# GpSimd's bias add behind the second power, VectorE's final add last in its step

## The chip, the core and the metric

The kernel runs on one core of one Trainium2 chip. The metric is device time in microseconds; before the change the median of three runs is 1020.15 us (1020.0 to 1021.33).

## What is computed

32 sequences of 512 tokens go through one block of a small language model with 256 channels:

```python
h = weight[x] * keep_mask[x]                       # gather 512 rows of 256, masked
# mixer on n1 = layernorm(h)
u, res = split(n1 @ in_proj_w.T)                   # 512 and 256 channels
u = conv1d(u, conv_w, 4 taps, causal) + conv_b
delta = softplus(u @ dt_proj_w.T + dt_proj_b)
g = u * sigmoid(delta)
y = scan(state = 0.9 * state + 0.1 * g)            # over the tokens
h = h + (y @ out_proj_w.T + res)
# quantised linear layer on n2 = layernorm(h)
xd = mx_quantise(n2)                               # blocks of 32, fp6 grid, dequantised
h = h + (xd @ wd.T + ffn_bias)
```

## The kernel before

Everything is float32. A product is made from three matmuls in fp32r: high part by high part, high by the low part of the weights, and the low part of the data by high. So each operand x of a product needs x_hi (a copy by ScalarE) and x_lo = x - x_hi (a subtraction, mostly on GpSimd: L370 for g, L377 for u, L407 for xT; VectorE makes nT_lo, L874).

The kernel is a software pipeline over the sequences, with an order written out by hand for every engine. Each engine has a function step(st) that is called for s = 0 to 33. In step s the "main" part works on sequence s (in_proj, convolution, dt_proj, gate), the "back" part on s - 1 (out_proj, scan, merge into h2, second norm, quantisation), the "tail" part on s - 2 (dequantise, turn by a DMA round trip through DRAM, linear product, bias, result, store). "front" prepares n1 of s + 1, "early" the statistics of s + 2. Engines wait for each other by semaphores only; each runs its own queue in order. Steps 2 to 29 have all of these parts; 30 has no "early" part, 31 neither "early" nor "front".

The places that matter here, by engine in the order of a step:

- GpSimd: first power (L384) and L386, g_lo[3] of s - 1 (L370), gathers, u_lo[0] and u_lo[1] (L377), gathers, **add_bias (L402)**, u_lo[2], u_lo[3], xT_lo (L407), second power inverse_root2 (L393, L396), g_lo[0] to g_lo[2].
- VectorE: dequantise (L769), turn_blocks (L862), gate(3) of s - 1 (L791), convolve (L707), turn_n1 (L869), scan (L799), convolve, add_h (L717) and statistics2, variance2 (L731, L734, L735), statistics1 (L838), variance1 (L845, L850, L851), gate(0), gate(1), **add_linear (L784)**, split_nT (L874), block_max (L740), quantise (L746, L754, L760), gate(2).
- ScalarE: taps, u_hi (L488), xT_hi (L550), tanh (L492), the second norm (L541, which waits for L396), g_hi (L499).
- TensorE: in_proj(0), (1), out_proj, in_proj(2), (3), dt_proj of m = 0, 1 for k = 0, 1 (L1026, L1027, L1033), merge (L1010 to L1017), dt_proj of m = 0, 1 for k = 2, 3, the linear product (L1070 to L1072, which waits for xT_lo), dt_proj(2) (its PSUM bank must have been read by gate(0)), dt_proj(3).

add_bias adds the bias in place to h2 of sequence s - 2; it waits for n2_ready of the step before (the norm has read h2). add_linear adds the linear product from PSUM (psO) to the same h2; it waits for bias_added and f_psum and releases result_ready, on which the output DMA of SyncE and the next step's merge wait.

Of the kernel before, what the change touches and what calls it, by code (L numbers as in the profile page):

```python
# [54 lines left out]
def lm_tower_kernel(nc, x, table, in_wT, conv_w, conv_b, dt_wT, dt_b, out_wT, ffn_w, ffn_b, turned, out):  # L55
# [13 lines left out]
    with ExitStack() as ctx:  # L69
# [131 lines left out]
        def f32(ap):  # L201
            return ap.bitcast(F32)
# [4 lines left out]
        def by_token(xT_part):  # L207

            return flat(xT_part).rearrange("p (m a i) -> p m a i", a=Q, i=BLOCK)

        def later(v):

            return not isinstance(v, int) or v > 0
# [32 lines left out]
        def span(part):  # L246

            return slice(0, C) if part is None else slice(part * C // 2, (part + 1) * C // 2)
# [8 lines left out]
        def linear_psum(st):  # L257


            return psZ_chunks if st.back and not st.main else psO  # L260
# [16 lines left out]
        def steps(eng, step):  # L277

            first = RING
            for s in range(0, first):  # L280
                step(Step(s, s % RING, s // RING))
            turns = (NSEQ - first - 2) // RING
            with eng.Fori(0, turns) as turn:
                for r in range(first, first + RING):
                    step(Step(RING * turn + r, r, turn + r // RING))
            for s in range(first + RING * turns, NSEQ + 2):
                step(Step(s, s % RING, s // RING))
# [54 lines left out]
        @block.gpsimd  # L342
        def _(pool):
            pool.memset(ident[:], 0.0).then_inc(zeroed, 1)
            pool.memset(decay[:], DECAY).then_inc(const_ready, 1)
            pool.memset(neg_half[:], -0.5).then_inc(const_ready, 1)
            pool.wait_ge(zeroed, 1)
            pool.affine_select(out=ident[:], in_=ident[:], compare_op=ALU.not_equal, fill=1.0, base=0,
                               pattern=[[-1, P]], channel_multiplier=1).then_inc(ident_ready, 1)

            def gather(b, ring, chunks):

                for c in chunks:
                    at = bass.IndirectOffsetOnAxis(ap=ids[:, b, c:c + 1], axis=0)
                    pool.indirect_dma_start(out=rows[:, ring, c, :], out_offset=None, in_=table,  # L355
                                            in_offset=at).then_inc(gathered[ring], 16)

            for n in range(2):
                pool.wait_ge(ids_loaded[n], 16)
                gather(n, n, range(C))  # L360
            pool.wait_ge(const_ready, 2)

            def step(st):
                s = st.s

                def split_g(m, s):
                    pool.wait_ge(g_hi_ready[m], s + 1)
                    if m == 0 and later(s):
                        pool.wait_ge(o_psum[1], s)
                    pool.tensor_tensor(g_lo[:, m, :], g[:, m, :], f32(g_hi[:, m, :]),  # L370
                                       ALU.subtract).then_inc(g_lo_ready[m], 1)

                def split_u(m):
                    pool.wait_ge(u_hi_ready[m], s + 1)
                    if m == 0 and later(s):
                        pool.wait_ge(z_psum[M - 1], s)
                    pool.tensor_tensor(u_lo[:, m, :], u[:, m, :], f32(u_hi[:, m, :]),  # L377
                                       ALU.subtract).then_inc(u_lo_ready[m], 1)

                def inverse_root1():  # L380
                    pool.wait_ge(var1_ready, s + 2)
                    if later(s + 1):
                        pool.wait_ge(n1_ready, s + 1)
                    pool.tensor_tensor(rstd1[:], ve1[:], neg_half[:], ALU.pow).then_inc(rstd1_ready, 1)  # L384
                    pool.wait_ge(rstd1_ready, s + 2)
                    pool.tensor_tensor(nmr1[:], nm1[:], rstd1[:], ALU.mult).then_inc(nmr1_ready, 1)  # L386

                def inverse_root2(part):
                    cs = span(part)
                    pool.wait_ge(var2_ready, s + (part or 0))  # L390
                    if later(s - 1):
                        pool.wait_ge(n2_ready, s - 1)
                    pool.tensor_tensor(rstd2[:, cs], ve2[:, cs], neg_half[:, cs],  # L393
                                       ALU.pow).then_inc(rstd2_ready, 1)
                    pool.wait_ge(rstd2_ready, s + (part or 0))
                    pool.tensor_tensor(nmr2[:, cs], nm2[:, cs], rstd2[:, cs], ALU.mult).then_inc(nmr2_ready, 1)  # L396

                def add_bias():
                    for part in st.tail_parts:
                        pool.wait_ge(n2_ready, s - 1 + (part or 0))  # L400
                        cs = h2[:, st.b, span(part)]
                        pool.tensor_tensor(cs, cs, bias[:].unsqueeze(1).to_broadcast([P, cs.shape[1], D]),  # L402
                                           ALU.add).then_inc(bias_added, 1)

                def split_xT():
                    pool.wait_ge(xT_hi_ready, s - 1)
                    pool.tensor_tensor(by_token(xT_lo[:]), xT_by_token, f32(by_token(xT_hi[:])),  # L407
                                       ALU.subtract).then_inc(xT_lo_ready, 1)

                if not st.main and st is not lead_in:  # L410
                    if st.back:
                        split_g(M - 1, s - 1)
                    add_bias()
                    if st.back:
                        for part in st.back_parts:
                            inverse_root2(part)
                    return

                if st.gather:
                    pool.wait_ge(ids_loaded[st.b], 16 * st.pair(2))  # L420
                    if later(s - 1):
                        pool.wait_ge(h2_ready[1], s - 1)
                if st.front:
                    inverse_root1()
                if st.back:
                    split_g(M - 1, s - 1)
                if st.gather:
                    gather(st.b, st.ring(2)[0], (0, 1))
                if st.main:
                    split_u(0)  # L430
                    split_u(1)
                if st.gather:
                    gather(st.b, st.ring(2)[0], (2, 3))
                if st.tail:
                    add_bias()
                if st.main:
                    split_u(2)
                    split_u(3)
                if st.tail:
                    split_xT()  # L440
                if st.back:
                    inverse_root2(None)
                if st.main:
                    split_g(0, s)
                    split_g(1, s)
                    split_g(2, s)

            step(lead_in)
            pool.wait_ge(dt_hi_ready, 1)
            pool.tensor_tensor(dt_lo[:], dt_stage[:], f32(dt_hi[:]), ALU.subtract).then_inc(dt_lo_ready, 1)  # L450
            pool.wait_ge(bias_loaded, 16)
            steps(pool, step)


# [172 lines left out]
        def _(dve):  # L627
# [66 lines left out]
            def step(st):  # L694
# [84 lines left out]
                def add_linear(part):  # L779

                    cs = span(part)
                    dve.wait_ge(bias_added, s - 1 + (part or 0))
                    dve.wait_ge(f_psum, s - 1 + (part or 0))
                    dve.tensor_tensor(h2[:, st.b, cs], h2[:, st.b, cs], linear_psum(st)[:, cs, :],  # L784
                                      ALU.add).then_inc(result_ready, 1)

                def gate(m, s=s):
                    dve.wait_ge(tanh_ready[m], s + 1)
                    if later(s):
                        dve.wait_ge(g_lo_ready[m], s)  # L790
                    dve.scalar_tensor_tensor(g[:, m, :], psZ[:, m % 2, :], 3.0, u[:, m, :], ALU.add,  # L791
                                             ALU.mult).then_inc(gated[m], 1)
# [119 lines left out]
                gate(1)  # L912
                if st.first:
                    choose_weight()
                if st.tail:
                    add_linear(None)
                if st.front:
                    split_nT()
                if st.back:
                    block_max(None)  # L920
                    quantise()
                    dve.wait_ge(q_ready, s)
                gate(2)
                if st.back and not st.front:
                    dequantise(None)

            step(lead_in)

            dve.wait_ge(small_loaded, 48)
# [244 lines left out]
```

## Time and profile before

| | |
|---|---|
| median of 3 runs | 1020.15 us |
| profiled execution | 1021.15 us, span 1019.3 us |
| TensorE busy | 956.8 us (94%) |
| VectorE busy | 946.7 us (93%) |
| ScalarE busy | 577.6 us (57%) |
| GpSimd busy | 721.3 us (71%) |
| granted clock of TensorE over the span | 0.991 |
| output DMA of one sequence, 512 KB, issue to landing, median | 2.9 us |
| HBM traffic | 99 GB/s over the span |

Times are microseconds. PE is TensorE, DVE is VectorE, ACT is ScalarE, POOL is GpSimd. A line of a timeline is: start, duration, engine, line of the kernel, operation, output<-input with partitions x elements, how many instructions are merged in it, and in brackets how long the engine was idle before it and who released it. A duration runs from the start of an instruction to its end, whatever it does in between.

### The profile page before, as it was taken

The page shows a single profiled execution, that of the slowest core. Times are in us where ns is not written, and L with a number is a line of the kernel's source. Part 1 is how long each engine was busy: PE and PEld are TensorE (multiplying, and loading weights), DVE is VectorE, ACT ScalarE, POOL GpSimd, SP SyncE. Part 2 cuts the span into 40 slices and gives each one's busy share as a digit, 9 for nine tenths or more (in the row PEclk, how much of TensorE's full clock was granted, in tenths as well). Part 3 has the DMA queues.
Part 4 walks back from the last instruction along what each step waited for, and adds up shares of the span by engine and source line. Part 5 has one row for each costly group of instructions (what it writes and reads, how often), then busy time and mean ns, then how long its engine had stood idle before and what let it go on. Part 6 is the DMA issues. An engine that isn't in the chain of part 4 may idle for free.

```text
span 1019.3 us, 14858 instructions
## 1 busy us (share of the span) xinstructions
PE 956.8 (94%) x4892; PEld 788.0 (77%) x4892; DVE 946.7 (93%) x1594; ACT 577.6 (57%) x966; POOL 721.3 (71%) x586
## 2 busy tenths in 40 slices
PE   3599999999999999999999999999999999999996
PEld 2377888788788888878887878878887888787885
DVE  4779999999999999999999999999999999999866
ACT  4455655655565665565565556566556556555441
POOL 5656777877677877677788767787767777876561
PEclk9899999999999999999999999999999999999998
DMA  4223323334323434333334432343433343442201
GB/s 150 62 63 95 90 86 105 116 112 125 95 81 92 124 103 124 107 86 95 103 105 122 123 93 78 97 124 103 124 103 86 96 106 103 124 124 84 77 28 41
DMA packets 73787, 100.78 MB, mean 99 GB/s; under 512 B 12576, under 2 KB 61088, under 8 KB 73760
## 3 DMA queue, kind: packets, MB, share of 16 engines
q1 hardware_dynamic: 67616, 83.59, 26.7%
q0 software_dynamic: 6144, 16.85, 7.5%
q8 instruction: 14, 0.23, 0.1%
q14 instruction: 13, 0.11, 0.0%
HBM read 51.65 MB, written 48.76 MB: 99 GB/s over the span
## 4 chain that ended last, share of the span: by engine, by line
PE 48%; POOL 26%; issue 14%; DVE 8%; ACT 4%; DMA 1%; POOLq 0%; DVEq 0%
POOL g_lo L370 7%; PE psZ L1033 6%; POOL u_lo L377 6%; POOL rows L355 6%; PE psZ L1026 6%; PE psZ L1027 5%; POOL h L402 3%; PE psT L984 3%; PE psU L969 3%; PE psT L980 3%; PE psU L965 3%; PE psT L981 3%; PE psU L966 3%; ACT n L541 2%; PE psO L1070 2%
## 5 line engine op out<-in xcount | busy, mean ns | idle before, releaser
L370 POOL TENSOR_TENSOR g_lo<-g,g_hi 128x512 fp32r<-128x512 f32 x128 | 201.6, 1586 | 210.4 <-ACT g_hi L499 210.4
L707 DVE SCALAR_TENSOR_TENSOR u<-psU,cw,u 128x511 f32<-128x511 f32 x378 | 258.2, 739 | 4.2 <-ACT u L481 1.5
L1026 PE MATMUL psZ<-u_hi,dt_hi 128*128 128x512 f32 x512 | 204.0, 399 | 12.8 <-ACT u_hi L488 6.8
L1033 PE MATMUL psZ<-u_lo,dt_hi 128*128 128x512 f32 x512 | 206.6, 404 | 6.7 <-POOL u_lo L377 5.6
L1027 PE MATMUL psZ<-u_hi,dt_lo 128*128 128x512 f32 x512 | 203.2, 397 | 0.0
L377 POOL TENSOR_TENSOR u_lo<-u,u_hi 128x512 fp32r<-128x512 f32 x128 | 163.0, 1296 | 11.4 <-ACT u_hi L488 10.6
L499 ACT ACTIVATE g_hi<-g 128x512 fp32r<-128x512 f32 x128 | 77.0, 625 | 132.0 <-DVE g L791 131.9
L355 POOL DMA_INDIRECT rows<-table,ids x128 | 126.1, 985 | 30.9 <-issue 29.6
L488 ACT ACTIVATE u_hi<-u 128x512 fp32r<-128x512 f32 x128 | 80.5, 629 | 109.9 <-DVE u L707 106.0
L1033 PEld LDWEIGHTS psZ<-u_lo,dt_hi 128*128 128x128 f32 x512 | 96.6, 189 | 44.5 <-POOL u_lo L377 21.9
L1026 PEld LDWEIGHTS psZ<-u_hi,dt_hi 128*128 128x128 f32 x512 | 96.8, 189 | 32.3 <-issue 7.2
L492 ACT ACTIVATE psZ<-psZ,gate_b 128x512 f32<-128x512 f32 x128 | 83.4, 653 | 66.7 <-PE psZ L1033 66.4
L481 ACT ACTIVATE u<-psU,cb,cw 128x512 f32<-128x512 f32 x126 | 94.6, 776 | 45.3 <-PE psU L969 40.6
L1027 PEld LDWEIGHTS psZ<-u_hi,dt_lo 128*128 128x128 f32 x512 | 96.9, 189 | 20.6
L965 PE MATMUL psU<-nT_hi,in_hi 128*128 128x512 f32 x252 | 100.8, 400 | 1.2 <-ACT nT_hi L561 1.2
L984 PE MATMUL psT<-g_lo,ow_hi 128*128 128x512 f32 x256 | 101.2, 395 | 0.6 <-POOL g_lo L370 0.6
L980 PE MATMUL psT<-g_hi,ow_hi 128*128 128x512 f32 x256 | 101.2, 395 | 0.0
L981 PE MATMUL psT<-g_hi,ow_lo 128*128 128x512 f32 x256 | 101.1, 395 | 0.0
L969 PE MATMUL psU<-nT_lo,in_hi 128*128 128x512 f32 x252 | 100.4, 398 | 0.0
L966 PE MATMUL psU<-nT_hi,in_lo 128*128 128x512 f32 x252 | 100.4, 398 | 0.0
L541 ACT ACTIVATE n<-h,nmr,rstd 128x256 f32<-128x256 f32 x128 | 66.7, 591 | 40.4 <-POOL nmr L396 40.4
L791 DVE SCALAR_TENSOR_TENSOR g<-psZ,u 128x512 f32<-128x512 f32 x128 | 84.3, 678 | 3.8 <-ACT psZ L492 2.5
(110 smaller groups left out, 2181.7 us busy)
## 6 DMA issues: line engine op xcount, KB each, us to landing
turned_n<-nb_blocks SPq DMA_DIRECT2D x31, 512.0 KB
nT<-turned_n SPq DMA_DIRECT2D x124, 128.0 KB
out<-h SPq DMA_DIRECT2D x31, 512.0 KB, 2.9
turned<-xb SPq DMA_DIRECT2D x30, 512.0 KB, 2.6
xT<-turned SPq DMA_DIRECT2D x120, 128.0 KB
rows<-table,ids POOLq DMA_INDIRECT x128
dt_stage<-dt_wT SPq DMA_DIRECT2D x1, 1024.0 KB, 5.7
g<-in_wT SPq DMA_DIRECT2D x1, 768.0 KB, 4.7
```

The source lines that it names most:

```text
L355: pool.indirect_dma_start(out=rows[:, ring, c, :], out_offset=None, in_=table, in_offset=at).then_inc(gathered[ring], 16)
L370: pool.tensor_tensor(g_lo[:, m, :], g[:, m, :], f32(g_hi[:, m, :]), ALU.subtract).then_inc(g_lo_ready[m], 1)
L377: pool.tensor_tensor(u_lo[:, m, :], u[:, m, :], f32(u_hi[:, m, :]), ALU.subtract).then_inc(u_lo_ready[m], 1)
L707: dve.scalar_tensor_tensor(u[:, m, back:T], u_psum_tile(st, m)[:, 0:T - back], cw[:, m, TAPS - 1 - back:TAPS - back], u[:, m, back:T], ALU ...
L965: pe.matmul(tile, in_hi[:, k, o], nT_hi[:, b, k, :], start=(k == 0), stop=False)
L966: pe.matmul(tile, in_lo[:, k, o], nT_hi[:, b, k, :], start=False, stop=False)
L980: pe.matmul(psY[:, d, :], ow_hi[:, k, o], g_hi[:, k, :], start=(k == 0), stop=False)
L981: pe.matmul(psY[:, d, :], ow_lo[:, k, o], g_hi[:, k, :], start=False, stop=False)
L984: ins = pe.matmul(psY[:, d, :], ow_hi[:, k, o], g_lo[:, k, :], start=False, stop=(k == M - 1))
L1026: pe.matmul(psZ[:, m % 2, :], dt_hi[:, k, o], u_hi[:, k, :], start=(k == 0), stop=False)
L1027: pe.matmul(psZ[:, m % 2, :], dt_lo[:, k, o], u_hi[:, k, :], start=False, stop=False)
L1033: ins = pe.matmul(psZ[:, m % 2, :], dt_hi[:, k, o], u_lo[:, k, :], start=False, stop=(k == M - 1))
```

## The change

GpSimd's add_bias moves from between the second pair of gathers and u_lo[2] to behind inverse_root2, ahead of g_lo[0]. VectorE's add_linear moves from between gate(1) and split_nT to the end of the step, behind gate(2). No operation is added or removed. The two steps without a main part (s = 32 and 33) are not touched.

```diff
@@ -431,8 +431,6 @@
                     split_u(1)
                 if st.gather:
                     gather(st.b, st.ring(2)[0], (2, 3))
-                if st.tail:
-                    add_bias()
                 if st.main:
                     split_u(2)
                     split_u(3)
@@ -440,6 +438,8 @@
                     split_xT()
                 if st.back:
                     inverse_root2(None)
+                if st.tail:
+                    add_bias()
                 if st.main:
                     split_g(0, s)
                     split_g(1, s)
@@ -912,8 +912,6 @@
                 gate(1)
                 if st.first:
                     choose_weight()
-                if st.tail:
-                    add_linear(None)
                 if st.front:
                     split_nT()
                 if st.back:
@@ -921,6 +919,8 @@
                     quantise()
                     dve.wait_ge(q_ready, s)
                 gate(2)
+                if st.tail:
+                    add_linear(None)
                 if st.back and not st.front:
                     dequantise(None)
```

## Rows read from the trace of the kernel before

**Rows 1.** Busy time in one step: stretch, length, each engine's busy time, clock, DMA.

```profile
466.55:496.70 30.15, 29.46 (x152) 24.34 (x152) 29.18 (x50) 17.98 (x31) 22.44 (x19) 1.00 0.36 105
```

**Rows 2.** Timeline of GpSimd, step 14, then steps 29 and 30.

```profile
461.67 2.41 POOL L402 TENSOR_TENSOR h<-h,bias 128x1024 f32<-128x1024 f32 x1
464.04 2.54 POOL L377 TENSOR_TENSOR u_lo<-u,u_hi 128x512 fp32r<-128x512 f32 x2
466.55 2.37 POOL L407 TENSOR_TENSOR xT_lo<-xT,xT_hi 128x1024 fp32r<-128x1024 f32 x1
470.23 0.20 POOL L396 TENSOR_TENSOR nmr<-nm,rstd 128x4 f32<-128x4 f32 x1
473.14 3.52 POOL L370 TENSOR_TENSOR g_lo<-g,g_hi 128x512 fp32r<-128x512 f32 x2 [2.71 <-ACT g_hi L499]
480.15 1.55 POOL L370 TENSOR_TENSOR g_lo<-g,g_hi 128x512 fp32r<-128x512 f32 x1 [3.49 <-ACT g_hi L499]
...
918.70 2.39 POOL L407 TENSOR_TENSOR xT_lo<-xT,xT_hi 128x1024 fp32r<-128x1024 f32 x1
...
945.25 1.30 POOL L377 TENSOR_TENSOR u_lo<-u,u_hi 128x512 fp32r<-128x512 f32 x1 [1.82 <-ACT u_hi L488]
...
947.97 2.41 POOL L407 TENSOR_TENSOR xT_lo<-xT,xT_hi 128x1024 fp32r<-128x1024 f32 x1
```

**Rows 3.** Timeline of TensorE around the linear product of step 14.

```profile
466.63 0.50 PE L1033 MATMUL psZ<-u_lo,dt_hi 128*128 128x512 f32 x1
...
469.02 0.36 PE L1070 MATMUL psO<-ffn_hi,xT_hi 128*128 128x256 f32 x1 [0.50 <-issue]
...
471.95 0.40 PE L1026 MATMUL psZ<-u_hi,dt_hi 128*128 128x512 f32 x1
```

**Rows 4.** Timeline of VectorE, second half of step 14, and one row of step 30.

```profile
467.38 1.57 DVE L734 TENSOR_SCALAR nm<-mv 128x4 f32<-128x4 f32 x1
...
470.85 0.17 DVE L850 TENSOR_SCALAR nm<-mv 128x4 f32<-128x4 f32 x1
...
471.00 1.28 DVE L791 SCALAR_TENSOR_TENSOR g<-psZ,u 128x512 f32<-128x512 f32 x2
472.22 1.22 DVE L784 TENSOR_TENSOR h<-h,psO 128x1024 f32<-128x1024 f32 x1
473.35 2.16 DVE L874 TENSOR_TENSOR nT_lo<-nT,nT_hi 128x1024 fp32r<-128x1024 f32 x1
...
478.72 0.69 DVE L791 SCALAR_TENSOR_TENSOR g<-psZ,u 128x512 f32<-128x512 f32 x1
479.33 1.22 DVE L769 SCALAR_TENSOR_TENSOR xd<-q,bscale 128x1024 f32<-128x1024 fp8e4 x1
...
953.66 1.22 DVE L784 TENSOR_TENSOR h<-h,psO 128x1024 f32<-128x1024 f32 x1 [1.86 <-PE psO L1072]
```

**Rows 5.** L734 (ns min/median/max of 33), and a VectorE and a GpSimd row at the start.

```profile
L734 DVE TENSOR_SCALAR nm<-mv x33: 169/1653/1789, 77.3 to 1002.3; 128x4 f32<-128x4 f32 x31, 128x2 f32<-128x2 f32 x2
...
23.14 4.56 DVE L850 TENSOR_SCALAR nm<-mv 128x4 f32<-128x4 f32 x1
...
23.06 4.61 POOL L450 TENSOR_TENSOR dt_lo<-dt_stage,dt_hi 128x2048 fp32r<-128x2048 f32 x1 [7.38 <-ACT dt_hi L462]
```

**Rows 6.** Timelines of VectorE and GpSimd in steps 0 and 1.

```profile
50.78 1.65 DVE L687 SCALAR_TENSOR_TENSOR h<-h,bscale 128x512 f32<-128x512 f32 x1
...
80.72 1.22 DVE L874 TENSOR_TENSOR nT_lo<-nT,nT_hi 128x1024 fp32r<-128x1024 f32 x1
...
83.10 1.27 DVE L746 TENSOR_SCALAR bscale<-amax 128x32 f32<-128x32 f32 x1
...
86.73 1.22 DVE L769 SCALAR_TENSOR_TENSOR xd<-q,bscale 128x1024 f32<-128x1024 fp8e4 x1
...
81.66 2.67 POOL L370 TENSOR_TENSOR g_lo<-g,g_hi 128x512 fp32r<-128x512 f32 x2 [2.71 <-ACT g_hi L499]
```

**Rows 7.** Timeline of ScalarE: u_hi[2] of step 14.

```profile
462.31 0.63 ACT L488 ACTIVATE u_hi<-u 128x512 fp32r<-128x512 f32 x1 [2.64 <-DVE u L707]
```

## The prediction

> **What bounds the kernel now.** I read the page's busy shares, then one step of the main loop in one row per engine, then the timelines of GpSimd (POOL) and VectorE (DVE) over that step. The step lasts 30.15 us at a granted clock of 1.00 (2.4 GHz) and has TensorE busy for 29.46 us and VectorE for 29.18 us [rows 1]. Its length repeats: the low part of xT starts at 918.70 in step 29 and at 466.55 in step 14, 452.15 / 15 = 30.14 us each [rows 1, 2]. So TensorE and VectorE are both nearly full, and the question is which busy time is work and which is waiting counted as busy.
>
> On GpSimd the reader sees the bias add (L402, 461.67) start as soon as the gathers are issued, and the low parts of u[2], u[3] (L377) and of xT (L407) queue behind it; L407 ends at 468.92 [rows 2]. Two TensorE holes hang on this. The first matmul on u_lo[2] starts at 466.63, just after u_lo[2] can be there, and the linear product L1070 starts after 0.50 us of idle time at 469.02, 0.10 us after L407 ends [rows 3]. The page calls that hole "issue"; by its time L407 is the releaser.
>
> On VectorE the reader should distrust two durations [rows 4]. L734 negates 128x4 means and is listed at 1.57 us, while its twin L850, same form, is listed at 0.17. L734 ends at 468.95, L407 at 468.92. It is no accident of one step: the median of 33 is 1.65 us, the minimum 0.17 [rows 5]. And L850 took 4.56 us at 23.14, ending 27.70, when GpSimd's L450 ran until 27.67 [rows 5]. So such an instruction waits until the GpSimd operation in progress has ended. L874 (two SBUF inputs) took 2.16 us beside g_lo, which began 0.21 us before it, and 1.22 us in the step where it began first; there g_lo waited instead (its pair is 2.67 us and ends at 84.33) [rows 2, 4, 6]. L687, a scalar_tensor_tensor with two SBUF inputs, shows the same: 1.65 us for 128x512 [rows 6]. The Trainium skill, page "SBUF — State Buffer", section "Who interferes with whom", has this as a rule: VectorE in a two-port mode, or with two SBUF inputs against a GpSimd operation that reads SBUF, and GpSimd exclude each other for a whole instruction, and the first to issue wins. The rows agree; the rule adds no price.
>
> **The change, first part: the bias add leaves its place.** Without L402 in the way, u_lo[2] starts when u_hi[2] is there: 462.31 + 0.63 = 462.94, plus a hand-off of 0.08 [rows 2, 7]. Step 30 shows the length of the chain with L402 out of the way, since there it had ended earlier: u_lo[2] starts at 945.25 and L407 ends at 947.97 + 2.41 = 950.38, 5.13 us later [rows 2]. So L407 would end at 463.02 + 5.13 = 468.15 instead of 468.92: 0.77 us earlier. L734 still waits for it (it asks at 467.38), and L735, the second power (L393), L396 and L838 all come 0.77 us earlier. Both holes of TensorE nearly close. That is the gain.
>
> **Second part: where the bias add lands.** L396 ends at 470.43, or 469.66 after the shift. The bias add waits only for n2_ready of the step before, long given, so it starts there and holds GpSimd for 464.04 - 461.67 = 2.37 us, until 472.03 [rows 2]. VectorE in that time asks for L850, at 470.85 - 0.77 = 470.08, 0.4 us after the bias add began [rows 4]. L850 has the form that waits. It ends at 472.06, not at 470.25, and gate(0), queued behind it, starts at 472.04 instead of 471.00: +1.04 us net of the 0.77 gained. Bounds for L850's wait: 0 if it got in first, 1.8 as worked out; I take 1.8, since a duration of this same instruction shows the wait. Behind L850 on VectorE are both gates; behind gate(0) is TensorE, whose dt_proj(2) starts at 471.95 today [rows 3] and could then start only near 472.75.
>
> **Third part: the final add last.** L784 takes 472.22 to 473.35, 1.13 us of VectorE's queue, wherever it stands [rows 4]; it has one SBUF input and one in PSUM. L874 then starts 1.22 us after gate(0), at 473.26 rather than 473.35. g_lo[0] starts 1.43 us after its gate (478.72 to 480.15 shows the distance) [rows 2, 4], at 473.47, so now L874 is first and runs in 1.22. This gain is given back: L746 (128x32) then falls on g_lo[1], as at 83.10, where it took 1.27 instead of 0.18. From L874 to L769 that step took 86.73 - 80.72 = 6.01 us, today's 5.98 [rows 4, 6]. With L784 in between, L769 asks at 473.26 + 6.01 + 1.13 = 480.40 instead of 479.33. Now gate(2) is no longer directly ahead of L769: it starts at 480.40 - 1.13 - 0.61 = 478.66, g_lo[2] starts at 480.09, and L769, two SBUF inputs, asks 0.31 us too late. Today it is the other way round, and g_lo[2] is the one that waits (1.55 us) [rows 2]. g_lo's hold is 0.94 + 0.21 = 1.15 us by L874's wait, so L769 waits 1.15 - 0.31 = 0.84 us. Bounds: 0 (it slips in) and 1.15; L687 is the nearest row, and I take 0.84. The page named above speaks here against the change as well; without its rule the 0.84 would be 0.
>
> The output DMA on SyncE's queue is issued when L784 has ended, so it moves from about 473.4 to about 480.4. It takes 2.9 us to land (page, DMA issues), and the next DMA on that queue (xb) comes behind L769 and L862, so not before 482.5. What of the two could overlap is at most 2.9 - 2.1 = 0.8 us of a transfer whose result is needed a third of a step later. I cost it at nothing; with that cover gone it is at most 0.8 us per step. The next merge waits for the final add as well, but comes behind in_proj and out_proj of the next step.
>
> **Sum.** L769's end moves by 1.07 + 0.84 = 1.91 us, and from L769 to the next u_hi[2] VectorE's queue is the same work. So a step is 32.06 us. TensorE doesn't lengthen it: it has 29.46 us of work in a step, and its dt_proj(2) comes 0.8 us later than today while VectorE comes 1.91 us later, so that it reaches the next merge ahead of VectorE [rows 1, 3]. L850 exists in the steps that prepare a sequence two ahead; with a bias add these are steps 2 to 29, 28 of them: 28 x 1.91 = 53.5 us. In steps 30 and 31 there is no L850, L784 waits 1.86 us for TensorE today (953.66) and would not at its new place, while L769 still pays: between -2 and +1 each, together -0.5 [rows 4]. So 1021.15 (profiled execution) + 53 = 1074, and since that execution lies 1.0 above the median of 1020.15: 1073 us.
>
> **Rivals.**
> (a) L850 waits as forecast, L769 does not: 28 x 1.07 = 30, so 1050. For it: the margin is only 0.31 us. Chance 0.14.
> (b) L850 gets in ahead of the bias add or isn't held, L769 is held. L874 at 471.45 would then run into the bias add until 472.03, so L769 asks at 472.03 + 7.14 = 479.17, -0.16, plus 0.84: 0.68 x 28 = 19, so 1039. Against it: the bias add leads L850 by 0.4 us in a chain that repeats. Chance 0.08.
> (c) The other side, faster. Neither is held: the step falls by 0.16 us or more, 28 x 0.16 = 5, so 1015; if no waiting between the two engines remains, VectorE drops out as a bound and what TensorE isn't busy today is gained, 30.15 - 29.46 = 0.69, 28 x 0.69 = 19, 1001. It decides from the point where the bias add begins after L850 has been issued (0.4 us later) and g_lo[2] after L769 (0.3 us later). For it: the bias add is off TensorE's path. Chance 0.05.
> (d) Held more often: an extra hold of 1.0 to 1.2 us per step, at L769 by the first power L384 or at L874 by g_lo[0] (margin 0.2 us): about 1074 + 28 = 1102. Against it: after g_lo[0] the waiting L874 came in ahead of the queued g_lo[1]. Chance 0.05.
> (e) Gains and waits cancel to within 0.2%: chance 0.03.
>
> **How the numbers follow.** The forecast has 0.65; its own spread is 1066 to 1082 (0.2 us per step either way). The range reaches down to include (a) and most of (b) and up past the forecast: 1040 to 1084. About 0.2% is what a measurement of this kernel can tell from no change. Faster 0.05, same 0.03, slower 0.92.
>
> **What the changed profile would show.** L850 with a median near 2.0 us (0.17: the second part is wrong); L734 near 0.9 instead of 1.65; L407 ending 5.1 us after u_lo[2] starts; L874 at 1.22 and L746 near 1.3; L769 near 2.06 instead of 1.22; L1026 of dt_proj(2) idle for 1.5 to 2 us behind gate(0); steps of 32.06 us. The prediction is wrong in size if only one of L850 and L769 is long, and in sign if neither is.

## The result

The changed kernel takes 1075.67 us (median of 4 runs, 1075.04 to 1076.13) against 1020.74 us before (median of 4, one run more than the 1020.15 above comes from): a ratio of 1.0532, 95% interval 1.0516 to 1.0548. That is 54.9 us or 5.3% slower; 1073 us was forecast. The granted clock is 0.99 in both profiled executions.

The page of the changed kernel, share of busy time:

```profile
PE 971.9 (91%) x4892; PEld 789.2 (74%) x4892; DVE 1007.2 (94%) x1594; ACT 583.2 (54%) x966; POOL 738.5 (69%) x586
```

VectorE is "busy" for 60 us more than before with the same 1594 instructions. Work hasn't been added, so instructions have become longer. Below, an instruction is called held when the profile counts it as running while it waits for an instruction of the other engine to end: a tiny one then ends just behind that one, a long one about its own length behind it. No row says what the two engines share; the rows say which instructions wait, and how long. Busy time in one step, from L407 to the next L407, in the columns of [rows 1]:

```profile
488.40:520.42 32.02, 29.96 (x154) 24.33 (x153) 31.27 (x50) 18.23 (x31) 23.09 (x19) 1.00 0.34 98
```

32.02 us against 30.15, and VectorE's busy time goes from 29.18 to 31.27. Over 26 steps the mean is 32.06 us against 30.17 (L862 at 120.34 and 953.93; before, at 118.08 and 902.58). The timeline of GpSimd in this step, which answers to [rows 2]:

```profile
487.16 1.29 POOL L377 TENSOR_TENSOR u_lo<-u,u_hi 128x512 fp32r<-128x512 f32 x1 [0.18 <-ACT u_hi L488]
488.40 2.40 POOL L407 TENSOR_TENSOR xT_lo<-xT,xT_hi 128x1024 fp32r<-128x1024 f32 x1
...
492.11 0.20 POOL L396 TENSOR_TENSOR nmr<-nm,rstd 128x4 f32<-128x4 f32 x1
492.26 2.38 POOL L402 TENSOR_TENSOR h<-h,bias 128x1024 f32<-128x1024 f32 x1
496.07 3.39 POOL L370 TENSOR_TENSOR g_lo<-g,g_hi 128x512 fp32r<-128x512 f32 x2 [1.44 <-ACT g_hi L499]
502.69 1.30 POOL L370 TENSOR_TENSOR g_lo<-g,g_hi 128x512 fp32r<-128x512 f32 x1 [3.22 <-ACT g_hi L499]
503.94 2.01 POOL L384 TENSOR_TENSOR rstd<-ve,neg_half 128x4 f32<-128x4 f32 x1
```

And VectorE's, which answers to [rows 4]:

```profile
489.84 0.99 DVE L734 TENSOR_SCALAR nm<-mv 128x4 f32<-128x4 f32 x1
...
492.73 1.94 DVE L850 TENSOR_SCALAR nm<-mv 128x4 f32<-128x4 f32 x1
...
495.85 1.21 DVE L874 TENSOR_TENSOR nT_lo<-nT,nT_hi 128x1024 fp32r<-128x1024 f32 x1
...
498.22 1.28 DVE L746 TENSOR_SCALAR bscale<-amax 128x32 f32<-128x32 f32 x1
...
501.86 1.21 DVE L784 TENSOR_TENSOR h<-h,psO 128x1024 f32<-128x1024 f32 x1
502.99 2.08 DVE L769 SCALAR_TENSOR_TENSOR xd<-q,bscale 128x1024 f32<-128x1024 fp8e4 x1
505.10 1.25 DVE L862 STREAM_TRANSPOSE xb<-xd 128x1024 f32<-128x1024 f32 x1
```

Read the two together by their ends. The bias add ends at 492.26 + 2.38 = 494.64, and L850, asked for at 492.73, ends at 494.67. g_lo[2] begins 0.30 us before L769, so L769 waits for it; L769's arrival then holds GpSimd's next operation, the power L384, so that it takes 2.01 us (median 1.01 before). The gain is there as well: L734 is down to 0.99.

### The profile page after: what moved, and what is told of

Same layout as the page of the kernel before. It is cut to its first block, busy times and chain, and to the rows that moved or that the text cites. A ratio compares the mean times of both kernels' runs of the same rounds, so it can differ in the third digit from the quotient of the medians.

```text
span 1073.6 us, 14858 instructions
## 1 busy us (share of the span) xinstructions
PE 971.9 (91%) x4892; PEld 789.2 (74%) x4892; DVE 1007.2 (94%) x1594; ACT 583.2 (54%) x966; POOL 738.5 (69%) x586
## 4 chain that ended last, share of the span: by engine, by line
DVE 38%; PE 32%; issue 18%; POOL 9%; ACT 2%; DMA 1%; DVEq 0%; POOLq 0%
DVE u L707 6%; POOL g_lo L370 5%; DVE stats L838 4%; DVE g L791 4%; PE psU L965 4%; DVE xd L769 3%; PE psZ L1026 3%; PE psZ L1027 3%; PE psZ L1033 3%; PE psO L1017 3%; PE psO L1016 3%; PE psU L969 3%; PE psO L1015 3%; PE psU L966 3%; PE psO L1010 3%
## 5 line engine op out<-in xcount | busy, mean ns | idle before, releaser
L370 POOL TENSOR_TENSOR g_lo<-g,g_hi 128x512 fp32r<-128x512 f32 x128 | 189.0, 1487 | 201.3 <-ACT g_hi L499 201.3
L1026 PE MATMUL psZ<-u_hi,dt_hi 128*128 128x512 f32 x512 | 207.4, 405 | 51.8 <-DVE g L791 44.8
L1033 PE MATMUL psZ<-u_lo,dt_hi 128*128 128x512 f32 x512 | 203.8, 398 | 0.1
L499 ACT ACTIVATE g_hi<-g 128x512 fp32r<-128x512 f32 x128 | 79.6, 632 | 179.2 <-DVE g L791 179.1
L1026 PEld LDWEIGHTS psZ<-u_hi,dt_hi 128*128 128x128 f32 x512 | 97.0, 190 | 79.4 <-DVE g L791 51.4
L481 ACT ACTIVATE u<-psU,cb,cw 128x512 f32<-128x512 f32 x126 | 97.7, 777 | 48.5 <-PE psU L969 43.8
L1033 PEld LDWEIGHTS psZ<-u_lo,dt_hi 128*128 128x128 f32 x512 | 96.9, 189 | 25.3 <-POOL u_lo L377 1.6
L984 PE MATMUL psT<-g_lo,ow_hi 128*128 128x512 f32 x256 | 104.2, 407 | 10.3 <-POOL g_lo L370 10.3
L965 PE MATMUL psU<-nT_hi,in_hi 128*128 128x512 f32 x252 | 103.6, 411 | 2.6 <-ACT nT_hi L561 1.2
```

Of the source, the lines that this page charges most:

```text
L965: pe.matmul(tile, in_hi[:, k, o], nT_hi[:, b, k, :], start=(k == 0), stop=False)
L984: ins = pe.matmul(psY[:, d, :], ow_hi[:, k, o], g_lo[:, k, :], start=False, stop=(k == M - 1))
L1026: pe.matmul(psZ[:, m % 2, :], dt_hi[:, k, o], u_hi[:, k, :], start=(k == 0), stop=False)
L1033: ins = pe.matmul(psZ[:, m % 2, :], dt_hi[:, k, o], u_lo[:, k, :], start=False, stop=(k == M - 1))
```

## Experiments

**Each move alone.** The first run moves only the bias add (the first two hunks of the diff), the second only the final add (the last two).

> Only GpSimd's bias add moves; VectorE's final add stays behind gate(1). Theory (an instruction of VectorE that needs what GpSimd holds waits for the whole GpSimd operation): L850 is held as in the changed kernel (1.94 us) and gate(0) comes 1.04 us later than before. The nT_lo subtraction L874 then asks 1.04 us later for what g_lo[0] holds, and its wait shrinks from 0.95 to about 0.2, so most of it is absorbed; the dequantisation L769 stays directly behind gate(2) and isn't held (1.22 us). Steps of about 30.6 us, 1030 to 1036 us. Rival (the two moves cost independently, so the bias add alone costs its 1.04 us in 28 steps): 1050 us. Rival (all of the cost comes from the final add): at or below 1005 us.

Measured: 1030.13 us, ratio 1.0083 (1.0067 to 1.0100). VectorE of this run:

```profile
506.10 1.95 DVE L850 TENSOR_SCALAR nm<-mv 128x4 f32<-128x4 f32 x1
...
509.23 1.21 DVE L784 TENSOR_TENSOR h<-h,psO 128x1024 f32<-128x1024 f32 x1
510.36 1.47 DVE L874 TENSOR_TENSOR nT_lo<-nT,nT_hi 128x1024 fp32r<-128x1024 f32 x1
...
515.53 1.22 DVE L769 SCALAR_TENSOR_TENSOR xd<-q,bscale 128x1024 f32<-128x1024 fp8e4 x1
```

L850 is held as long as with both moves, yet the run is only 8.8 us slower than before. The delay of gate(0) is eaten up by L874, which comes later and so waits 0.26 instead of 0.95 us. A held instruction is slack for what comes ahead of it. The step is 30.34 us (from L769 to L769, 485.19 to 515.53); the mean of 26 is 30.45. Here VectorE does wait a little for TensorE's merge, 18.3 us in 51 waits, against 4.5 us in 19 before:

```profile
DVE h L717 <- PE psO L1017: 18.3, 51, 0.5
...
L734 DVE TENSOR_SCALAR nm<-mv x33: 168/264/621, 77.9 to 1012.7; 128x4 f32<-128x4 f32 x31, 128x2 f32<-128x2 f32 x2
```

L734 has a median of 0.26 us against 0.99 in the changed kernel, because VectorE comes to it later, after waiting for the merge.

> Only VectorE's final add moves; the bias add stays ahead of u_lo[2]. Theory: L850 stays at 0.17 and L734 at 1.65; L874 is now ahead of g_lo[0] (1.21), L746 is held instead (1.28), and g_lo[2] begins ahead of L769, which is held for 0.84 us (2.07). A step grows by about 0.87 us: 1044 to 1049 us. Rival (the order of the final add is free, the whole cost is the bias add's): 1020 us, within 0.3%.

Measured: 1046.7 us, ratio 1.0247 (1.0230 to 1.0265).

```profile
512.42 0.17 DVE L850 TENSOR_SCALAR nm<-mv 128x4 f32<-128x4 f32 x1
...
513.77 1.22 DVE L874 TENSOR_TENSOR nT_lo<-nT,nT_hi 128x1024 fp32r<-128x1024 f32 x1
...
516.15 1.28 DVE L746 TENSOR_SCALAR bscale<-amax 128x32 f32<-128x32 f32 x1
...
519.78 1.21 DVE L784 TENSOR_TENSOR h<-h,psO 128x1024 f32<-128x1024 f32 x1
520.91 2.07 DVE L769 SCALAR_TENSOR_TENSOR xd<-q,bscale 128x1024 f32<-128x1024 fp8e4 x1
```

The final add alone, a reordering with no operation added, costs 25.4 us: L769 is held in every step, and L746 has taken over L874's wait. The mean step is 0.91 us longer (0.87 expected). The sum of the two runs is 8.8 + 25.4 = 34 us, the two moves together cost 54.9 us. Most of the missing 21 us is L874's wait: the bias add alone used up 0.69 us of it in each of 28 steps, 19 us. With both moves the final add has already exchanged it for L746's, and nothing absorbs the delay.

**The dequantisation ahead of the final add.** To the changed kernel:

```diff
-                    dequantise(None, own=False)     # first in the next step
...
                 gate(2)
+                if st.back:
+                    dequantise(None)
                 if st.tail:
                     add_linear(None)
-                if st.back and not st.front:
-                    dequantise(None)
```

> Both moves, but the dequantisation L769 comes directly behind gate(2), ahead of the final add (before it was the first instruction of the next step, so the order of the queue is gate(2), L769, L784, L862). Theory: L769 is again ahead of g_lo[2] and takes 1.22 instead of 2.08; g_lo[2] waits instead (1.55); L850 is still held. A step falls by 0.84 us against the changed kernel, 1048 to 1053 us. Rival (L769's length comes from the load on memory at that time or from the output DMA, not from the order): 1075 us, and L769 stays near 2 us.

Measured: 1045.97 us, ratio 1.0248 (1.0221 to 1.0274), 29.7 us below the changed kernel. The mean step is 31.07 us, 0.99 less. L769 takes 1.22 in this run, and g_lo[2] waits for it:

```profile
520.76 1.22 DVE L769 SCALAR_TENSOR_TENSOR xd<-q,bscale 128x1024 f32<-128x1024 fp8e4 x1
521.59 1.54 POOL L370 TENSOR_TENSOR g_lo<-g,g_hi 128x512 fp32r<-128x512 f32 x1 [3.22 <-ACT g_hi L499]
521.89 1.21 DVE L784 TENSOR_TENSOR h<-h,psO 128x1024 f32<-128x1024 f32 x1
```

So L769 is long only behind g_lo[2]. By itself this run doesn't exclude the output DMA: it is issued at 503.24 in the changed kernel, 0.25 us after L769 has begun, and here only at 523.27, after L769 has ended. The run with the final add one instruction back settles it below. The run is 2 us faster than the range: a step is 0.99 us shorter, not 0.84. The spacing explains it. L769 to L862 was 2.11 us in the changed kernel and 1.25 before (479.33 to 480.58), 0.86 more, as forecast (0.84); but L769 to L784 is only 1.13, since L784 doesn't need what L769 has written, while L862 does.

**The bias add later still, behind VectorE's L851.** To the changed kernel:

```diff
                 if st.tail:
+                    if st.early:
+                        pool.wait_ge(var1_ready, s + 3)
                     add_bias()
```

> Both moves, but GpSimd's bias add waits also until VectorE has done L850 and L851, so it begins some 0.8 us later. Theory (who issues first holds the other for a whole operation): L850 falls from 1.94 to 0.17; gate(0) comes 1.77 us earlier; but L874 now asks while the bias add runs and is held for about 1.3 us (2.5 us in all), so that only about 0.4 us per step is won: 1061 to 1068 us. Rival (L850 is the only instruction that the bias add holds): a step 1.8 us shorter, about 1025 us. Rival (overlap slows both in proportion): L850 and the bias add both near their lengths alone whatever the order, 1075 us.

Measured: 1061.07 us, ratio 1.0395 (1.0377 to 1.0412); the bias add begins 0.74 us after GpSimd has come free. Lines of VectorE are two higher in this kernel (L852 is L850, L876 is L874):

```profile
515.80 0.17 DVE L852 TENSOR_SCALAR nm<-mv 128x4 f32<-128x4 f32 x1
...
516.12 2.41 POOL L402 TENSOR_TENSOR h<-h,bias 128x1024 f32<-128x1024 f32 x1 [0.74 <-DVE ve L853]
517.15 2.47 DVE L876 TENSOR_TENSOR nT_lo<-nT,nT_hi 128x1024 fp32r<-128x1024 f32 x1
518.49 3.54 POOL L370 TENSOR_TENSOR g_lo<-g,g_hi 128x512 fp32r<-128x512 f32 x2
```

The same two operations, with the order of their starts reversed: L850's form goes from 1.94 to 0.17. The hold isn't gone, it has found another instruction: L874 ends at 519.62, 1.09 us after the bias add (518.53), and is 1.26 us longer than in the changed kernel. Of the 1.77 us won at L850, 0.51 us per step remain. This rules out slowing in proportion, and it rules out L850 as the only victim.

**The bias add in two halves.** To the changed kernel: two instructions of 128x512 in place of one of 128x1024.

> Both moves, the bias add as two instructions of 128x512 one behind the other. Theory (the hold lasts for one GpSimd instruction, and a waiting instruction comes in at its end): L850 falls from 1.94 to about 0.9 us. What L851 and the gates then meet decides the rest: if the second half comes in between L850 and L851, L851 waits about 1.2 us and the time stays at 1075 us; if L850 and L851 both go before it, about 1.0 us per step is won, 1045 to 1052 us. Rival (GpSimd's work slows VectorE for as long as it runs): L850 stays near 1.9 us, 1075 us.

Measured: 1045.6 us, ratio 1.0240 (1.0219 to 1.0260). L857 is L850, L858 is L851 here:

```profile
510.14 2.53 POOL L405 TENSOR_TENSOR h<-h,bias 128x512 f32<-128x512 f32 x2
...
510.61 0.84 DVE L857 TENSOR_SCALAR nm<-mv 128x4 f32<-128x4 f32 x1
511.37 0.16 DVE L858 TENSOR_SCALAR ve<-mv 128x4 f32<-128x4 f32 x1
```

L850 ends at 511.45, the first half of the bias add at about 511.4 (half of 2.53 after 510.14). L851 begins at 511.37, at the boundary of the two halves, and isn't held either. 1.1 us per step is won with the bias add in the same place: here the wait lasts until the end of the one GpSimd instruction in progress, not until GpSimd is idle.

**What was there to be gained.** The kernel before, with the bias add of the main steps over 4 of 256 channels of one chunk at its old place:

```diff
-                        cs = h2[:, st.b, span(part)]
+                        cs, bs = h2[:, st.b, span(part)], bias[:]
+                        if st.main:
+                            cs, bs = h2[:, st.b, 0:1, 0:4], bias[:, 0:4]
```

> The kernel before, with the bias add of the steps with a main part at its old place but over one chunk and 4 of 256 channels (the rest of the bias is left out of the result). It measures what the change was after: the queue of GpSimd without the bias add ahead of u_lo[2]. Theory: L407 ends 0.77 us earlier, L734 falls from 1.65 to about 0.9 us, nothing else is held, TensorE's holes ahead of the linear product nearly close; steps of about 29.4 us, 997 to 1003 us. Rival (VectorE or TensorE is the bound whatever GpSimd does there): 1015 us or more.

Measured: 999.8 us, ratio 0.9795 (0.9776 to 0.9814). L734's form has a median of 0.88 us, and a step is 29.48 us (L862's form at 499.52 and 529.00; the mean of 26 is 29.39). So the first half of the change aimed at something real, about 21 us. This run leaves out most of GpSimd's work on the bias, so it doesn't tell how much of the gain a mere change of place would bring.

**The same place in the queue, with two gathers in it.** The kernel before, with the bias add where the first pair of gathers was, and those gathers, for the sequence after, behind the second power:

```diff
-                if st.gather:
+                if st.gather and st.first:
                     gather(st.b, st.ring(2)[0], (0, 1))
+                if st.tail:
+                    add_bias()
...
-                if st.tail:
-                    add_bias()
                 if st.main:
                     split_u(2)
...
+                if st.load:
+                    pool.wait_ge(ids_loaded[st.nb], 16 * st.pair(3))
+                    if later(s):
+                        pool.wait_ge(h2_ready[1], s)
                 if st.back:
                     inverse_root2(None)
+                if st.load:
+                    gather(st.nb, st.ring(3)[0], (0, 1))
```

> The kernel before, with GpSimd's queue in another order: the bias add takes the place of the first pair of gathers (between g_lo[3] and u_lo[0], while VectorE convolves, with nothing of it that can be held), and the first pair of gathers of the next sequence goes behind the second power, where the change had put the bias add. The final add stays. Theory: u_lo[2], u_lo[3] and xT_lo come 0.77 us earlier as in the run with a tiny bias add, L734 falls to about 0.9 us, and the gathers there hold L850 for at most 0.2 us (0.37 us beside a gather at 12.11 in the kernel before): steps of about 29.5 us, 998 to 1004 us. Rival (gathers behind the second power hold VectorE's L850 as the bias add did): L850 near 1 us, 1020 us or more.

Measured: 1005.56 us, ratio 0.9849 (0.9829 to 0.9868): 1.5% faster than before, but 1.6 us above the range. L850 (L856 here) isn't held beside the gather. What the expectation missed is L874 (L880), which now asks just 0.06 us after g_lo[0] instead of 0.21, and takes 2.31 us. Its median is 0.15 us above that of the run with the tiny bias add, and the mean step 0.22 us (29.61 against 29.39). The other 0.07 are one step in which L880 took 4.26 us, 1.94 above its median (the last section has the rows):

```profile
521.82 1.03 POOL L355 DMA_INDIRECT rows<-table,ids  x1 [0.15 <-issue]
521.92 0.17 DVE L856 TENSOR_SCALAR nm<-mv 128x4 f32<-128x4 f32 x1
...
524.38 3.53 POOL L370 TENSOR_TENSOR g_lo<-g,g_hi 128x512 fp32r<-128x512 f32 x2 [0.29 <-ACT g_hi L505]
524.44 2.31 DVE L880 TENSOR_TENSOR nT_lo<-nT,nT_hi 128x1024 fp32r<-128x1024 f32 x1
```

**The final add one instruction back, not six.** The kernel before, and the last run, with add_linear directly behind split_nT:

```diff
-                if st.tail:
-                    add_linear(None)
                 if st.front:
                     split_nT()
+                if st.tail:
+                    add_linear(None)
```

> The kernel before with this alone: VectorE's final add directly behind split_nT, nothing moved on GpSimd. It is the same add as in the change, set back by one instruction instead of by seven. Theory: L874 1.21 instead of 2.16, L746 up to 0.3, L769 still first behind gate(2) (1.22), L850 0.17; VectorE gains 0.8 to 0.95 us per step until TensorE binds: 996 to 1003 us. Rival (setting the final add back costs as in the run with the final add alone): 1035 to 1047 us. Rival (without the bias add out of the way, TensorE's wait for xT_lo keeps the step at 30.15 us): 1018 to 1022 us.

Measured: 996.55 us, ratio 0.9757 (0.9735 to 0.9778), 24 us less, with nothing else changed. In the fence SPq is the DMA queue of SyncE; the row is the issue of the output DMA.

```profile
519.24 1.22 DVE L874 TENSOR_TENSOR nT_lo<-nT,nT_hi 128x1024 fp32r<-128x1024 f32 x1
520.18 2.68 POOL L370 TENSOR_TENSOR g_lo<-g,g_hi 128x512 fp32r<-128x512 f32 x2 [2.71 <-ACT g_hi L499]
520.37 1.22 DVE L784 TENSOR_TENSOR h<-h,psO 128x1024 f32<-128x1024 f32 x1
521.50 1.21 DVE L740 TENSOR_REDUCE amax<-n 128x32 f32<-128x1024 f32 x1
521.87 0.41 SPq L334 DMA_DIRECT2D out<-h  x1
522.75 0.18 DVE L746 TENSOR_SCALAR bscale<-amax 128x32 f32<-128x32 f32 x1
...
523.52 1.22 DVE L760 SCALAR_TENSOR_TENSOR q<-n,brecip 128x1024 fp8e4<-128x1024 f32 x1 [0.20 <-DVE brecip L754]
```

L874 goes ahead of g_lo[0]; then the two g_lo run while VectorE does L784 and L740, which they don't hold; when L746 comes at 522.75, they are done but for 0.1 us (522.86). Both waits are gone. TensorE's wait for xT_lo is nearly gone too, with the bias add still in its old place (0.8 us in 3 waits at L1070, 12.7 us in 26 before). And the rows answer the rival of the output DMA: it is issued at 521.87 and takes 2.9 us to land (median), and L760 runs within that time in 1.22 us. Like L769 it is a scalar_tensor_tensor of 128x1024 with two inputs in SBUF, and it can be held: it takes 1.80 us in step 30 of the changed kernel (1010.69), beside g_lo[1]. The transfer under way doesn't make it long. The change sets the same add back by six instructions (the expectation says seven), and that was the 25 us loss of the second run.

> As the run with the gathers ahead, and VectorE's final add goes one instruction back, from ahead of split_nT to behind it. Theory: L874 then starts at or ahead of g_lo[0] and isn't held (1.21 instead of 2.3 us), and the 2.4 us in which g_lo[0] and g_lo[1] run are filled with the final add and the block maximum, neither of which is ever held, so that L746 meets at most the end of g_lo[1] (0.2 to 0.4 us). VectorE has 1 us to spare per step and TensorE is the bound with its 29.2 us: 993 to 999 us. Rival (holds are only moved on, L746 takes 1.28 as in the changed kernel): 1003 to 1008 us.

Measured: 987.36 us, ratio 0.9672 (0.9658 to 0.9687), 3.3% faster than the kernel before and 88 us faster than the changed one. It is 6 us below the range. One line tells why, busy time over the stretch 134 to 918:

```profile
134.00:918.00 784.00, 784.00 (x4127) 664.13 (x4126) 728.57 (x1327) 482.48 (x810) 581.42 (x484) 1.00 0.35 108
```

TensorE is busy for all of it. A step is 29.03 us (L713, the convolution, at 500.89 and 529.92), the mean of 26 is 28.94; I had put TensorE's floor at 29.2. L734 (L740 here) has a median of 0.17 us in this run: VectorE waits for the merge, so it asks for L734 later, when L407 has ended.

## Why the prediction was right

- Sign and mechanism: right. The step was forecast at 32.06 us and measured at 32.06 (mean of 26). Rivals (a), (b) and (c) fall, since both L850 and L769 are held in the changed kernel. (d) falls, since L874 takes 1.21 us and L769 no more than 2.08. (e) falls by the time.
- The gain: as forecast, L407 ends 5.1 us after u_lo[2] starts (485.69 + 5.11 = 490.80). L734 was forecast near 0.9 and measured at 0.99. The tiny bias add shows the gain, 21 us, when nothing takes it back. Only one of TensorE's two holes closed, though, where the prediction has both nearly closed: the wait for u_lo at L1033 (4.6 us in 19 waits before) is gone from the waits view, but L1070 still stands idle for 0.31 us (0.5 before) and starts 0.10 us after L407's end:

```profile
490.90 0.36 PE L1070 MATMUL psO<-ffn_hi,xT_hi 128*128 128x256 f32 x1 [0.31 <-issue]
```

- L850: forecast 1.8 us of wait, measured 1.94 - 0.17 = 1.77. The late start and the halves show that the order of starts decides it, and the end of the one instruction in progress.
- L874 and L746: the exchange that was read off step 1 [rows 6] came as forecast, 1.21 and 1.28.
- L769: forecast 2.06, measured 2.08; putting it ahead of the final add, so ahead of g_lo[2], brings it back to 1.22.
- L1026: forecast 1.5 to 2 us idle behind gate(0). The waits view of the changed kernel has 1.4:

```profile
PE psZ L1026 <- DVE g L791: 36.4, 26, 1.4
```

TensorE stood still a little less there and some elsewhere (it also waits for g_lo now, 8.8 us in 26 waits at L984). It made no difference to the end.
- What was short: 53 us forecast against 54.9 measured. The starts of L769 in the two traces show where. At the end of step 29 the changed kernel is 52.4 us behind (983.84 against 931.40; 53.5 forecast), at the end of step 31 it is 54.7 us behind (1042.87 against 988.16). The mis-sized term is that of steps 30 and 31: -0.5 together in the prediction, +2.3 in the traces. As forecast, L784 no longer waits for TensorE there. But VectorE now waits for the second norm instead, 2.21 us at L740 in step 30. About 1 us of this is a hold in the other direction: L874 came 0.06 us ahead of GpSimd's L396, which the norm needs, and L396 took 1.22 us instead of 0.20:

```profile
1004.88 1.21 DVE L874 TENSOR_TENSOR nT_lo<-nT,nT_hi 128x1024 fp32r<-128x1024 f32 x1
1004.94 1.22 POOL L396 TENSOR_TENSOR nmr<-nm,rstd 128x4 f32<-128x4 f32 x1
...
1008.30 1.22 DVE L740 TENSOR_REDUCE amax<-n 128x32 f32<-128x1024 f32 x1 [2.21 <-ACT n L541]
```

In step 31 L740 waits 1.58 us for the norm, without such a hold. So the forecast of the total is somewhat nearer than its terms: one is 1.1 us too high and the other 2.8 us too low.
- Behind the prediction, two sizes were off. TensorE's floor per step was taken as 29.2 us and is 28.94, so the last run went below its range. And the wait for g_lo at L874 in the run with the gathers ahead depends on the lead between the two to a tenth of a microsecond, which the expectation ignored.

## What to carry to other kernels

A queue order on GpSimd is also a schedule for VectorE: before moving an operation on either, list which instructions of the other engine run beside it and which of them need what it holds. Counting inputs doesn't find them: L734, L850 and L746 read a single tile in SBUF and are held, as L874 and L769 are with two. Place GpSimd's long operations beside VectorE work that the traces show unheld (here the convolution, the adds with an input in PSUM, the block maximum), and give the instruction of VectorE that can be held the start ahead of GpSimd's rather than just behind. A tiny instruction with a long duration in a timeline is suspect; compare its end with the end of what the other engine is doing.

## What the runs showed that I had not expected

- The waits are slack that can be spent once. The two moves cost 8.8 and 25.4 us alone and 54.9 together.
- An instruction that has waited mostly goes ahead of the next one in the other engine's queue: L850 was done at the boundary of the two halves of the bias add, and L769 went ahead of L384 (median of 32 now 2.01 us, 1.01 before). There is one exception in the traces: in the run with the gathers ahead, L874 (L880) asked once while a gather ran and then waited for both g_lo. It ends at 794.50, 1.09 us after them. Why it didn't come in between them, no run shows.

```profile
789.88 0.96 POOL L355 DMA_INDIRECT rows<-table,ids  x1 [1.21 <-issue]
790.24 4.26 DVE L880 TENSOR_TENSOR nT_lo<-nT,nT_hi 128x1024 fp32r<-128x1024 f32 x1
790.87 2.54 POOL L370 TENSOR_TENSOR g_lo<-g,g_hi 128x512 fp32r<-128x512 f32 x2
```

- GpSimd's gathers did not hold L850: it took 0.17 us beside one (521.92), though they ran in the slot in which the bias add had held it for 1.77. That isn't general: at the start of the kernel before, L850 asked while a gather was running and ended 0.01 us before it.

```profile
11.54 0.95 POOL L355 DMA_INDIRECT rows<-table,ids  x1 [0.30 <-issue]
12.11 0.37 DVE L850 TENSOR_SCALAR nm<-mv 128x4 f32<-128x4 f32 x1
```
